# Attention operands placed from SBUF, ScalarE in the recurrent stage, two expert layers interleaved

## What is computed

```python
# 1 attention, 16 heads of d = 8, causal, with a linear bias by distance
q, k, v = split(x @ W_attn.T)
att = softmax(q @ k.T / sqrt(8) + slope[h] * (pos_k - pos_q), causal)
x = x + (att @ v) @ W_proj.T
# 2 expert choice: each of 8 experts takes its 256 best tokens
scores = softmax(xf @ router_w + router_b)        # of 8192 tokens
G, idx = top_k(scores.T, 256)
h1 = relu(xf[idx] @ w1 + b1); eo = h1 @ w2 + b2
y.at[idx].add(eo * G)
# 3 gated convolution and linear recurrence
u, v = split(x @ in_proj_w + in_proj_b); v_local = dwconv3(silu(v))
h = a * h + ssm_b * v_local; y = ssm_c * h + ssm_d * v_local   # along the positions
out = (u * silu(y)) @ out_proj_w + out_proj_b
x = x + layernorm(out + normed_x) * ln_w + ln_b
# 4 top-2 of 8 experts (gated, width 352) behind an RMS norm
x = x + sum_e w_e * ((silu(y @ W1_e) * (y @ W2_e)) @ W3_e) + (the layer's own input)
```

## Time and profile before

| stage | from, to | length | PE | DVE | ACT | POOL | PEclk | DMA |
|---|---|---|---|---|---|---|---|---|
| attention | 0, 820 | 820 | 685.97 | 554.54 | 386.87 | 177.85 | 0.96 | 0.32 |
| project | 820, 928 | 108 | 74.27 | 64.63 | 10.78 | 36.08 | 0.52 | 0.48 |
| choose | 928, 1004 | 76 | 9.07 | 55.30 | 15.29 | 0.00 | 0.50 | 0.02 |
| expert choice | 1004, 1090 | 86 | 40.41 | 7.76 | 15.60 | 57.09 | 0.80 | 0.38 |
| mixer | 1090, 1320 | 230 | 106.10 | 199.76 | 56.57 | 123.96 | 0.58 | 0.14 |
| gate, dispatch | 1320, 1430 | 110 | 43.57 | 85.57 | 38.44 | 47.32 | 0.50 | 0.20 |
| experts of layer 4 | 1430, 1909 | 479 | 426.60 | 310.40 | 215.46 | 375.63 | 0.98 | 0.32 |

### The profile page before, as it was taken

One profiled execution on the slowest core, in us unless ns is written; L12 is line 12 of the kernel. 1 busy time (PEld: TensorE's weight loads), 2 busy tenths in 40 slices (PEclk: granted clock), 3 DMA queues, 4 the chain that ended last, 5 costly groups with the idle time before them and its releaser, 6 DMA issues. The chain is left out here.

```text
span 1909.6 us, 33952 instructions
## 1 busy us (share of the span) xinstructions
PE 1386.0 (73%) x9370; PEld 869.1 (46%) x9371; DVE 1278.0 (67%) x3736; ACT 739.0 (39%) x1489; POOL 817.9 (43%) x716
## 2 busy tenths in 40 slices
PE   1788889889888988949315254541809999999996
PEld 0355445555555545438204222221806556555654
DVE  4667667667677766738671189998686666666664
ACT  0255445445555555511212132222424444444443
POOL 3222222222222222024006546565616888888886
PEclk9999899999999999965557765565559999999999
DMA  3533333233233233136104300030032333333332
GB/s 76 133 73 71 63 74 80 64 75 81 74 74 72 72 72 74 39 125 220 43 0 112 63 30 22 16 112 6 22 163 38 41 43 42 42 41 43 41 42 35
DMA packets 72986, 124.48 MB, mean 65 GB/s; under 512 B 17888, under 2 KB 42272, under 8 KB 70480
## 3 DMA queue, kind: packets, MB, share of 16 engines
q0 software_dynamic: 39168, 59.42, 18.6%
q1 hardware_dynamic: 25728, 51.42, 8.3%
q10 hardware_dynamic: 8032, 12.93, 1.9%
HBM read 65.25 MB, written 57.94 MB: 65 GB/s over the span
## 5 line engine op out<-in xcount | busy, mean ns | idle before, releaser
L425 DVE TENSOR_REDUCE mx<-psS 128x1 f32<-128x384 f32 (+3 forms) x704 | 428.2, 638 | 222.5 <-PE psS L319 211.9
L486 ACT ACTIVATE probs<-psE 128x1024 f32<-128x1024 f32 (+2 forms) x384 | 326.7, 884 | 290.3 <-PE psE L335 289.2
L316 PE MATMUL psS<-maskq,identb 128*128 128x128 bf16 (+2 forms) x704 | 178.5, 254 | 109.4 <-DMA kop<-qkv_scr 88.3
L1804 POOL DMA_INDIRECT out<-ex_y,ex_idx x144 | 235.8, 1638 | 48.6 <-issue 42.6
L319 PE MATMUL psS<-kop,qop 96*128 96x128 bf16 (+3 forms) x1024 | 246.5, 309 | 0.0
L335 PE MATMUL psE<-qop,kop 128*128 128x512 bf16 (+3 forms) x1024 | 231.4, 307 | 0.0
L332 PE MATMUL psE<-maskk,identb 128*128 128x128 bf16 (+2 forms) x704 | 175.0, 249 | 2.5 <-ACT probs L486 2.5
L344 PE MATMUL psY<-probs,vaug 128*32 128x512 f32 (+3 forms) x2048 | 176.5, 455 | 0.0
L1795 POOL DMA_INDIRECT ex_xg<-expert_tab,ex_idx x144 | 141.8, 985 | 66.2 <-issue 42.1
L316 PEld LDWEIGHTS psS<-maskq,identb 128*128 128x128 bf16 x704 | 67.8, 98 | 204.2 <-DVE mx L425 81.7
L1778 DVE SCALAR_TENSOR_TENSOR ex_h<-ex_psG,ex_w,ex_up 128x352 f32<-128x352 f32 x144 | 84.1, 584 | 109.9 <-ACT ex_w L1879 107.7
(11 more groups left out here) (309 smaller groups left out, 2669.9 us busy)
## 6 DMA issues: line engine op xcount, KB each, us to landing
y_scr<-ysb SPq DMA_DIRECT2D x64, 256.0 KB, 2.2
qkv_scr<-parts POOLq DMA_DIRECT2D x32, 384.0 KB, 3.4
qop<-qkv_scr POOLq DMA_DIRECT2D x16, 384.0 KB, 5.8
kop<-qkv_scr POOLq DMA_DIRECT2D x16, 384.0 KB, 6.5
expert_tab<-table_rows SPq DMA_DIRECT2D x1, 4352.0 KB, 14.5
qop<-qkv_scr POOLq DMA_DIRECT2D x16, 256.0 KB, 7.2
kop<-qkv_scr POOLq DMA_DIRECT2D x16, 256.0 KB, 8.3
pj_num<-y_scr SPq DMA_DIRECT2D x16, 256.0 KB
```

The lines of the kernel that those rows point to most:

```text
L316: pe.matmul(out[:, :, P * j:w], identb[:], maskq[:, 0:nh, :], start=True, stop=False, skip_group_check=True)
L425: dve.tensor_reduce(mx[:, j, h0:h0 + nh], psS[u % 2][:, 0:nh * w].rearrange("p (h k) -> p h k", h=nh), AX, ALU.max).then_inc(s_su, 1)
L486: act.activation(dst, src, ACT.Exp).then_inc(s_ex, 1)
L1804: pool.indirect_dma_start(out, bass.IndirectOffsetOnAxis(ap=idx[t % 8][:], axis=0), y[m][:], None, compute_op=ALU.add).then_inc(s_sc[m], 16)
```

## The change

**Attention.** The DRAM scratch qkv_scr, keep_part and the semaphore s_pw go. place waits for both low parts (s_lo) and then issues twelve transfers, one of q and one of k for each of the six products, from 128 partitions of parts (each partition one 1 KB row) into 8 partitions of qop or kop. ScalarE's hi_part, which overwrites the parts, waits for the operands to be placed (s_op) where it waited for the stores. TensorE waits for 12 transfers a batch where it waited for 6.

```diff
-            def keep_part(n, b, s):
-
-                if s == 0 and b >= 2:
-                    pool.wait_ge(s_op, 16 * 6 * (b - 1))
-                pool.wait_ge(s_lo, 2 * b + s + 1)
-                pool.dma_start(qkv_scr[n, s].rearrange("a p q -> p a q"), parts[s][:]).then_inc(s_pw, 16)
-
             def place(n, b):
 
-                pool.wait_ge(s_pw, 32 * b + 32)
                 if b >= 2:
                     pool.wait_ge(s_er, EN * G * (b - 1))
-                row = 0
-                for k in (3, 2, 1):
-                    w = 8 * k
-                    q_src = qkv_scr[n, 0, 0:k].rearrange("a (d h) q -> (a d) (h q)", d=D)
-                    pool.dma_start(qop[n][row:row + w].rearrange("p h q -> p (h q)"), q_src).then_inc(s_op, 16)
-                    k_src = qkv_scr[n, 1, 3 - k].rearrange("(d h) q -> d (h q)", d=D)
-                    pool.dma_start(kop[n][row:row + w].rearrange("p h q -> p (h q)"), k_src.unsqueeze(0).to_broadcast([k, D, H * T]))\
-                        .then_inc(s_op, 16)
-                    row += w
+                pool.wait_ge(s_lo, 2 * b + 2)
+                for row, (of_q, of_k) in enumerate(TERMS):
+                    here = slice(D * row, D * row + D)
+                    pool.dma_start(qop[n][here], parts[0][:, of_q, :]).then_inc(s_op, 16)
+                    pool.dma_start(kop[n][here], parts[1][:, of_k, :]).then_inc(s_op, 16)
...
-                act.wait_ge(s_pw, 32 * b)
+                if not isinstance(b, int) or b:
+                    act.wait_ge(s_op, 16 * 12 * b)
```

```diff
+            turn(0)
+            pe.wait_ge(s_b, 64)
             for e in range(E):
-                body(e % 2, e, e == E - 1)
+                if e + 1 < E:
+                    turn(e + 1)
+                first(e)
+                if e:
+                    second(e - 1)
+            second(E - 1)
...
+                dve.tensor_tensor(lg[:], psL[n].rearrange("p (h e) -> p h e", h=2), rbs[:], ALU.add).then_inc(s_g, 1)
...
+                dve.tensor_reduce(top[:], lg[:], AX, ALU.max).then_inc(s_g, 1)
...
+                dve.tensor_tensor(lg[:], lg[:], top[:].unsqueeze(2).to_broadcast([P, 2, E]), ALU.subtract).then_inc(s_g, 1)
+                dve.wait_ge(s_ex, e + 1)
+                dve.tensor_reduce(tot[:], ex[:], AX, ALU.add).then_inc(s_g, 1)
...
+                dve.reciprocal(tot[:], tot[:]).then_inc(s_g, 1)
...
+                dve.tensor_tensor(score[n][:], ex[:, :, e], tot[:], ALU.mult).then_inc(s_g, 1)
```

```diff
+                    act.wait_ge(s_r, s + 1)
+                    if not isinstance(s, int) or s >= 2:
+                        act.wait_ge(s_tr, s - 1)
+                        act.wait_ge(s_xo, s - 1)
+                    for t in range(TT):
+                        i = act.activation(xn[n][:, t], x_tile(s, t), ACT.Identity, bias=shift[:, t:t + 1], scale=rstd[:, t:t + 1])
+                    i.then_inc(s_xn, 1)
...
+                if live(s - 2, nb):
+                    b = s - 2
+                    act.wait_ge(s_r, s + 2)
...
+                        i = act.activation(hn[n][:, t], ho[n][:, t], ACT.Identity, bias=shift[:, u:u + 1], scale=rstd[:, u:u + 1])
+                    i.then_inc(s_hn, 1)
...
-                pool.tensor_tensor(rstd[:, cols], nrm.veps[:, cols], mhalf[:, cols], ALU.pow).then_inc(s_r, 1)
+                pool.tensor_tensor(rstd[:, cols], veps[:, cols], mhalf[:, cols], ALU.pow).then_inc(s_p, 1)
+                pool.wait_ge(s_p, s + 2)
+                pool.tensor_tensor(shift[:, cols], minus[:, cols], rstd[:, cols], ALU.mult).then_inc(s_r, 1)
```

More of the change, by code:

```diff
@@ L977, in expert_choice @@
         xg = sb("xg", [P, 2 * E, C], F32)
-        gg = sb("gg", [P, 2 * E * E], F32)
+        rws = sb("rws", [P, E], F32)
+        rbs = sb("rbs", [P, 2, E], F32)
+        lg, ex = (sb(n, [P, 2, E], F32) for n in ("lg", "ex"))
+        top, tot = (sb(n, [P, 2], F32) for n in ("top", "tot"))
+        score = [sb(f"score{i}", [P, 2], F32) for i in range(2)]
         w1s = [sb(f"w1s{i}", [P, FT * P], F32) for i in range(2)]
@@ L1068, in body @@
                 act.wait_ge(s_tr, e + 1)
-                act.activation(xT[n][:], psX[n][:], ACT.Copy).then_inc(s_xT, 1)
+                if e >= 2:
+                    act.wait_ge(s_h, e - 1)
+                act.activation(xT[n][:], psX[n][:, 0:2 * P], ACT.Copy).then_inc(s_xT, 1)
+            act.wait_ge(s_b, 64)
+            copy(0)
+            for e in range(E):
+                n = e % 2
+                if e + 1 < E:
+                    copy(e + 1)
+                act.wait_ge(s_g, SCORE * e + 3)
+                act.activation(ex[:], lg[:], ACT.Exp).then_inc(s_ex, 1)
@@ L1346, in step @@
                        .then_inc(s_y, 1)
[L1347 to L1355 removed]
+                if live(s + 2, nb):
+                    x_stats(s + 2, n)
                 if live(s - 1, nb):
@@ L1892, in dram @@
         return nc.dram_tensor(name, shape, dt).ap()
-    qkv_scr = dram("qkv_scr", [2, 2, 3, P, T], BF16)
     y_scr = dram("y_scr", [nb, H, 32, T])
```

251 lines of the change are left out of this document (143 added, 108 removed).

## The result

The changed kernel took 1947.62 us (median of four runs, 1942.70 to 1952.05) against 1907.44 before (four runs): a ratio of 1.0215, 95% interval 1.0173 to 1.0257, about 2% slower. The profiled execution took 1946.14 us, with a span of 1944.3 and a mean granted clock of 0.839; against the 1911.37 before that is +34.8, where the prediction's sum was +44 (the medians differ by 40).

What follows compares the result with a forecast made beforehand. Attention was taken as bound by the leg from finished parts to TensorE's next batch. Attention +85, recurrent stage -42, expert choice +1.5 and projection -0.4 gave +44, 1955.5 us profiled, 1950 as median; range 1828 to 2000.

Steps and rivals of the forecast that it cites:

- The bound of attention and its leg: Attention: the time from finished parts to TensorE's next batch sets the stage, growing from 24.6 to 29.9 us; +85 us.
- Longer waits for the placement, near 9 to 10 us a batch: Attention: TensorE's waits for the last operand transfer grow from 4.2 to some 9.6 us a batch.
- Every new transfer is as narrow, and q and k of one term go into the same 8 partitions: Attention: reason for taking 57 GB/s as the nearest row, 27.6 us for a batch's transfers.
- rival 2: Attention: rate stays near 87 to 100 GB/s and only the DRAM bounce goes; total -93, 1812 us; chance 0.15.
- Consecutive terms overlap a little: Attention: transfers of successive terms overlap as the six do now, so 26 us is taken where 57 GB/s gives 27.6.
- Rival 3: Attention: no narrow limit, leg under 20.4 us, -75; total -116, 1789 us; chance 0.07.
- Recurrent stage: Recurrent stage: a step falls from 13.42 to 10.2 us over 13 steps, -42 us, bounds -54 and -22.
- the forecast's own loop of ScalarE: Recurrent stage: ScalarE's way from normalised x through the second Silu and eight Identities, with hand-overs, takes 9.7 us a step.
- below both: Recurrent stage: GpSimd's 8.3 us a step lies below VectorE's loop of 9.3 and ScalarE's of 9.7.
- The collisions: Recurrent stage: VectorE operations with two SBUF operands stretch beside GpSimd; one a step gives 10.2 us, three give 11.7.
- Rival 5: Recurrent stage: gains nothing as GpSimd and VectorE exclude each other throughout; +42, 1992 us with the forecast; one in 12.
- Expert choice: Expert choice: weights requested after a second product make a cycle of 7.9 us; +1.5 us, bounds -12.5 and +8.

Runs made afterwards that it cites:

- dram_narrow: Changed kernel with the stores to qkv_scr of before and the twelve narrow transfers read from DRAM in rows of 16 KB; 1999.71 us (one run).
- q_then_k: Changed kernel with GpSimd issuing the six transfers of q first, then the six of k; 1811.04 us (one run).
- stride12: Changed kernel with the 8 rows of a term on every twelfth partition of qop and kop; 1799.73 us, ratio 0.9456 to the kernel before.
- hn_one_op: Changed kernel with ScalarE's second normalisation in the recurrent stage as one instruction over 512 columns, for timing only; 1941.78 us, step 9.68 us.
- no_t2: Changed kernel without GpSimd's addition of x and the bias row in each recurrent step, for timing only; 1938.39 us, step 9.36 us.

## Why the prediction was right, point by point

- **The bound of attention and its leg: right.** Forecast: leg 29.9 us, batches 52 to 53 apart, some 60 GB/s, +80 and +5. Measured: 28.8, 52.4, 67 in all or 62 for the placement's own bytes, +75.3 and +5.0. The step that gave it, taking the narrow stretch at 57 GB/s as the nearest row and not the mean of 87 to 100 or the 154, is what dram_narrow confirms with the source held as before.
- **"Longer waits for the placement, near 9 to 10 us a batch": wrong in its parts.** The later waits for it are (70.0 - 30.6) / 15 = 2.6 us a batch, and 4.4 are for the row maxima. The sum, 7.0, is 2.6 less than forecast, but the batches are only 0.3 shorter than its 52.7: TensorE's products take 1.1 us a batch more than before (16.5 / 15), and its waits for VectorE's maxima 1.1 more (16.6 / 15). The slow starts that the prediction left out of its sum ("up to +1 us a batch") are there, and a leg 1.1 us shorter than forecast hides them in the total (a batch is 28.8 + 23.6 us, where the forecast had 29.9 + 22.8). That is luck. The prediction had looked at the rate of the placement, and not at who else uses the queues it fills.
- **"Every new transfer is as narrow, and q and k of one term go into the same 8 partitions": more right than it knew.** It was said in passing, and it carries the whole loss: q_then_k, which changes that alone, gives the 1811 us that rival 2 was priced at (1812), by its rate too, 100 GB/s, and in attention, which ends 55.5 us before that of the kernel before (765.1), where it said 52. "Consecutive terms overlap a little" held only because the order was q, k, q, k. Rival 2 was put as a matter of row length; it was one of order.
- **Rival 3** (no narrow limit) was priced at 1789, and stride12 at 1799.7 is nearly it, with the limit avoided and not absent: the end of attention falls from 820.7 to 755.5, 65 less, where it said 75.
- **Recurrent stage: right in sign, short in size, for a reason that fails.** Forecast -42 (10.2 a step), measured -51.9 and +1.6 at the start. The step of 9.6 lies at the forecast's own loop of ScalarE, 9.7, and it is not that loop: hn_one_op. The term that was mis-sized is GpSimd, put at 8.3 "below both" (its own terms add up to 8.0); it is busy 8.86, and waits for veps besides. The collisions, put at one of 0.8 us a step, are some 0.8 on the taps (2.26 against twice 0.73) and 0.6 on the small instructions (1.96 against 1.34 in no_t2), and they are part of a loop with GpSimd and no price on top of VectorE's own. Rival 5, that the stage gains nothing, is out; but what it was about, the two engines holding one another up, is what sets the new step.
- **Expert choice: the wait was right, the size not.** Forecast +1.5, measured +5.7, within its upper bound of +8, by the mechanism named there. TensorE's first product does wait for ec_w2s, and then runs at the lower clock in four of five cases, 3.62 or 3.78 us where the sum had 1.99. The pairs of scatters come 7.1 to 10.2 us apart, not 7.9 (the last pair 5.9).
- **The sum:** 44 forecast, 34.8 measured. Attention gave 5 less, the recurrent stage 8 less, the stretch between 0.7 less, expert choice 4 more. That the sum is within 10 us owes something to terms that missed in opposite directions.

## What to carry to other kernels

Price a transfer by the partitions it lands in and by what is in flight beside it: if rows may stand in any order, put those of one transfer far apart, and if they may not, issue next to one another what goes to different groups. Look for who else issues into the queues that a slower transfer fills, since a 4 KB row behind it can hold the next engine. Where the instructions of two engines hold one another up in a loop, shorten the one that is busy longest and test it by taking work away, before a sum that happens to fit is believed.

## What the runs showed of the hardware

- The order of the same twelve transfers changed their rate from 67 to 100 GB/s, and the kernel by 135 us.
- Two transfers of one row of 4 KB each took 14 us while the 16 DMA engines were full of another queue's packets (issue 445.49, release 459.53), and did not hold TensorE where a placement of the same bytes into the same partitions loaded half of the engines (dram_narrow).
- A VectorE instruction over 8 columns with two operands in SBUF took 1.24 to 1.28 us beside a GpSimd sum or product, ending with it, where 0.17 is usual. The Trainium skill (SBUF — State Buffer, "Who interferes with whom") says that a VectorE instruction with two SBUF inputs contends with a GpSimd instruction that reads SBUF, and the trace agrees: in all twelve steps of the changed kernel a small instruction ends within 0.04 us behind GpSimd's sum. That moving the GpSimd instruction only hands its place to the next was not expected.
